# A decoder layer on one core: the final scatter in 28 tiles of 128 partitions instead of 32 of 112, with the read-back of the expert outputs in two parts

## The chip, the cores and the metric

The kernel runs on one core of one Trainium2 chip. The metric is the time of one execution in device microseconds (us). The profile is that of one execution, and its span runs from its first to its last instruction.

## What is computed

The input x has 16 batches of 224 tokens with 512 values. Three blocks are added to it: a bilinear causal mixer, a cross attention over 750 context rows with 16 heads, and a mixture of experts in which each of 32 experts picks 8 tokens of each batch. The change touches the last block alone, and of it the end:

```
probs = softmax(logits over the tokens); vals, idx = top_k(probs, 8)      # for each batch and expert
merged[b, e] = sum over k of vals[b, k, e] * x[b, idx[b, k, e]]
h = gelu([merged, 1] @ w1[e]);  o = [h, 1] @ w2[e]                        # w1[e] 513x2048, w2[e] 2049x512
out_tok[b, k, e] = o[b, e] * vals[b, k, e]
out[b, idx[b, k, e]] += out_tok[b, k, e];   x = x + out
```

Written as a product, batch b of the result is x[b] + router[b]^T @ o[b], where router[b] is 32 x 224 (the weight of each expert at each token, zero where it was not picked) and o[b] is 32 x 512.

## The kernel before

The program has three blocks: a setup, a pipeline over the 16 batches (mixer, attention, router and merging) and the experts. The last one is of interest here. `ring` is one buffer of 8 slots, each 128 partitions x 16 KB. An expert's weights are 8 MB and come in four chunks of 2 MB, one slot each: q 0 and 1 are w1, q 2 and 3 are w2. The even experts use slots 0 to 3, the odd ones slots 4 to 7. All loads are issued by SP (SyncE), whose queue is in order: a wait in it holds up everything behind it. The chunks of the last expert, 31, are issued by `weights(end, 1, ...)` in two pieces, and between them stand the 16 loads that bring x (kept in `out` by the pipeline) into the slots 0 to 3, which expert 30 has done with.

For each expert, TensorE (PE) multiplies the merged tokens by w1 (line 1573), transposes (1586), multiplies by w2 (1600) and sums four row groups (1558); VectorE (DVE) adds the bias row into `o_fin` (1515), which holds 16 rows (one for each batch) of 512. GpSimd (POOL) stores `o_fin` of the experts 0 to 30 into the DRAM tensor `o_rows` (1438, semaphore `o_stored`), and so turns rows by batch into rows by expert.

After the last expert comes the tail. SP reads `o_rows` back into `o_in` (1423), four DMAs of 31 partitions: partition r*32 + e of `o_in` holds the output of expert e for the batches 4g + r, g from 0 to 3. The row of expert 31 goes straight from `o_fin` into `o_in` in four DMAs of 4 partitions (1428). PE waits for all eight (`o_loaded`) and for `picks` (the router table in the same layout, 1407). Then it makes 32 products of 32 x 112 by 32 x 512 (1621), two for each batch: even tokens and odd tokens. The four batches of a group lie in four row groups of 32 partitions. DVE adds each product to x in the ring (1538), and ACT (ScalarE) issues one store of 112 partitions x 4 KB for each batch when both its halves are there (1472).

All three engines and the queues are ordered by semaphores as written; no scheduler moves anything.

Of the kernel before, what the change touches and what calls it, by code (L numbers as in the profile page):

```python
# [19 lines left out]
ALU = mybir.AluOpType  # L20
# [3 lines left out]
P = 128  # L24
# [48 lines left out]
def build(nc, x, ctx_in, aWq, aWk, aWo, U_b, V_b, W_b, bias_b, U_t, V_t, W_t, X_t, bias_t, alpha,  # L73
          xWq, xWkv, xWo, gate_w, gate_b, w1, w2, out):
    B, T, D = x.shape
    _, S, DC = ctx_in.shape
    R = V_b.shape[1]
    E, _, H = w1.shape
# [4 lines left out]
    TT = T // 2  # L83
# [43 lines left out]
    es = ExitStack()  # L127
    with es:
        def sem(name):
            return es.enter_context(nc.semaphore(name))  # L130

        def sb(stack, name, shape, dt=F32):
            return stack.enter_context(nc.sbuf_tensor(name, shape, dt))

        bank = [es.enter_context(nc.psum_tensor(f"bank{i}", [P, BANK], F32)) for i in range(8)]
        router = nc.dram_tensor("router", [B, E, T], F32).ap()
        o_rows = nc.dram_tensor("o_rows", [B, E, D], F32).ap()
# [291 lines left out]
        ring = sb(es, "ring", [P, SLOTS, 2 * H])  # L429
# [126 lines left out]
        def tokens(cols, t):  # L556

            return cols.rearrange("p (n t) -> p t n", t=2)[:, t, :]
# [792 lines left out]
        RW = 4  # L1351
        GB = B // RW
        o_in = sb(es, "o_in", [P, GB, D])
        picks = sb(es, "picks", [P, GB, T])

        b1_flipped = sem("b1_flipped")
        b1_ready = sem("b1_ready")
        cleared = sem("cleared")
# [13 lines left out]
        picks_loaded = sem("picks_loaded")  # L1372
        o_loaded = sem("o_loaded")
        fin_loaded = [sem(f"fin_loaded{g}") for g in range(GB)]
        scat_full = sem("scat_full")
        fin_ready = sem("fin_ready")
        fin_stored = sem("fin_stored")

        def fin(b):

            return ring[0:TT, b // RW, b % RW * 2 * D:(b % RW + 1) * 2 * D].rearrange(
                "p (t n) -> p t n", t=2)

        with nc.Block() as block:
            @block.sync
            def _(sp):
                def weights(i, e2, first, qs=range(4)):

                    e = i * 2 + e2
                    for q in qs if not first else ():  # L1390
                        slot = e2 * 4 + q
                        if q < 2:
                            sp.wait_ge(h_full, i * 2 + (e2 - 1))
                        else:
                            sp.wait_ge(o_full, i * 2 + (e2 - 1))
                        load_chunk(sp, e, q, slot)
                    if 3 not in qs:
                        return
                    if not first:
                        sp.wait_ge(o_out, i * 2 + (e2 - 1))  # L1400
                    sp.dma_start(b2_row[:, e2, :],  # L1401
                                 w2[bass.ds(e, 1), H1, :].to_broadcast([B, D])
                                 ).then_inc(b2_loaded[e2], 16)

                weights(0, 0, True)
                weights(0, 1, True)
                sp.dma_start(picks[:], router.rearrange("(g r) e t -> (r e) g t", r=RW)
                             ).then_inc(picks_loaded, 16)
                with sp.Fori(1, E // 2 - 1) as i:
                    weights(i, 0, False)  # L1410
                    weights(i, 1, False)
                end = E // 2 - 1
                weights(end, 0, False)
                weights(end, 1, False, (0, 1))
                for b in range(B):
                    if b % RW == 0:
                        sp.wait_ge(h_full if b < B // 2 else o_full, E - 1)
                    sp.dma_start(fin(b), out[b, :, :].rearrange("(p t) d -> p t d", p=TT)  # L1418
                                 ).then_inc(fin_loaded[b // RW], 16)
                weights(end, 1, False, (2, 3))  # L1420
                sp.wait_ge(o_stored, 16 * (E - 1))
                for r in range(RW):
                    sp.dma_start(o_in[r * E:(r + 1) * E - 1, :, :],  # L1423
                                 o_rows.rearrange("(g r) e n -> r e g n", r=RW)[r, 0:E - 1, :, :]
                                 ).then_inc(o_loaded, 16)
                sp.wait_ge(o_out, E)
                for g in range(GB):
                    sp.dma_start(o_in[E - 1:P:E, g, :], o_fin[g * RW:(g + 1) * RW, 1, :]  # L1428
                                 ).then_inc(o_loaded, 16)

            @block.gpsimd
            def _(pool):
                nc.gpsimd.memset(tok[:], 0.0).then_inc(cleared, 1)

                def keep_rows(i, e2):
                    e = i * 2 + e2
                    pool.wait_ge(o_out, i * 2 + (e2 + 1))
                    pool.dma_start(o_rows[:, bass.ds(e, 1), :].rearrange("b o n -> b (o n)"),  # L1438
                                   o_fin[:, e2, :]).then_inc(o_stored, 16)

                with pool.Fori(0, E // 2 - 1) as i:
                    keep_rows(i, 0)
                    keep_rows(i, 1)
                keep_rows(E // 2 - 1, 0)
                pool.wait_ge(o_stored, 16 * (E - 1))

            @block.scalar
            def _(act):
# [18 lines left out]
                with act.Fori(1, E // 2) as i:  # L1467
                    hidden(i, 0, False)
                    hidden(i, 1, False)
                for b in range(B):  # L1470
                    act.wait_ge(fin_ready, 2 * b + 2)
                    act.dma_start(out[b, :, :].rearrange("(p t) d -> p t d", p=TT), fin(b)
                                  ).then_inc(fin_stored, 16)
                act.wait_ge(fin_stored, 16 * B)

            @block.vector
            def _(dve):
# [51 lines left out]
                    add_biases(i, 1, False)  # L1529
                row_out(E // 2 - 1, 1, False)  # L1530

                for b in range(B):
                    g, r = b // RW, b % RW
                    if r == 0:
                        dve.wait_ge(fin_loaded[g], 16 * RW)
                    for t in range(2):
                        dve.wait_ge(scat_full, g * 2 * RW + t * RW + r + 1)
                        nc.vector.tensor_tensor(fin(b)[:, t, :], fin(b)[:, t, :],  # L1538
                                                bank[t * RW + r][0:TT, :], ALU.add
                                                ).then_inc(fin_ready, 1)  # L1540

            @block.tensor
            def _(pe):
# [66 lines left out]
                    expert(i, 1, False)  # L1610
                sum_parts(E // 2 - 1, 1, False)

                pe.wait_ge(picks_loaded, 16)
                pe.wait_ge(o_loaded, 16 * (RW + GB))
                for g in range(GB):
                    for t in range(2):
                        for r in range(RW):
                            if g:
                                pe.wait_ge(fin_ready, (g - 1) * 2 * RW + 2 * r + t + 1)
                            rows = slice(r * E, (r + 1) * E)  # L1620
                            nc.tensor.matmul(bank[t * RW + r][0:TT, :],  # L1621
                                             tokens(picks[rows, g, :], t), o_in[rows, g, :],
                                             start=True, stop=True).then_inc(scat_full, 1)


# [25 lines left out]
```

## Time and profile before

| | |
|---|---|
| time, median of 3 runs | 2379.69 us (2370.84, 2379.69, 2379.73) |
| time of the profiled execution | 2371.13 us |
| its span | 2369.5 us |
| busy: PE, DVE, ACT, POOL | 82%, 41%, 32%, 35% |
| experts' block begins | 1658.3 us |
| last expert's output row complete | 2308.0 us |
| first scatter product | 2339.4 us |
| last addition ends | 2363.6 us |

Times in the trace are counted from the span's start. A busy share is a mean over stages with different limits, so for a change in one stage the rows of that stage are what matters. "SPq" and "ACTq" are the DMA issues of those engines; a merged row of the timeline gives start, duration of the whole stretch, and the count. A tile's number is left out in the profile (`b_row` is `b2_row`, `bank` any bank of PSUM), and one product in f32 appears as two records.

### The profile page before, as it was taken

Reading aid. Unit: us, or ns where it says so; the run is one execution under the profiler, and the core shown is the slowest. Engines: PE = TensorE matmul, PEld = TensorE weight load, DVE = VectorE, ACT = ScalarE, POOL = GpSimd, SP = SyncE. Lnnn points to the kernel's source line nnn. Section 1 sums busy time; section 2 is a strip of 40 time slices with the busy share of each in tenths; the row PEclk is TensorE's granted clock in tenths of the full one; section 3 lists DMA queues with packets and bytes.
Section 4 is the critical chain, followed back from the end, with each engine's and each line's share of the span. In section 5 each row is a group of like instructions: output and inputs, shape, how many; then the busy total and the mean of one; then the engine's idle time right before and its main releaser. Section 6 shows DMA issues by size and latency. Waiting matters only on the chain. (4 is left out here: it accounts for less than half of the span.)

```text
span 2369.5 us, 39997 instructions
## 1 busy us (share of the span) xinstructions
PE 1953.3 (82%) x11970; PEld 1146.6 (48%) x11970; DVE 974.9 (41%) x2477; ACT 754.6 (32%) x1551; POOL 826.8 (35%) x592
## 2 busy tenths in 40 slices
PE   7789999999999999999999999986755655655633
PEld 5466666666666666666666666653211111111101
DVE  0355655656556556565565565651100000000003
ACT  2143434435444344354443443532100000000000
POOL 0245545555555455555554555543000000000000
PEclk8899999999999999999999999987877777777765
DMA  5223333242233332422433324263999999999974
GB/s 159 56 74 93 77 87 84 72 101 64 74 94 78 86 84 72 102 64 72 96 77 83 84 73 103 65 227 115 370 423 419 421 422 420 423 420 420 422 261 136
DMA packets 135414, 419.34 MB, mean 177 GB/s; under 512 B 32612, under 2 KB 74820, under 8 KB 110804
## 3 DMA queue, kind: packets, MB, share of 16 engines
q1 hardware_dynamic: 130292, 410.08, 50.9%
q10 hardware_dynamic: 4096, 7.80, 1.0%
q0 software_dynamic: 992, 1.02, 0.1%
q8 instruction: 19, 0.31, 0.1%
q14 instruction: 15, 0.12, 0.0%
HBM read 306.39 MB, written 16.15 MB: 136 GB/s over the span
## 5 line engine op out<-in xcount | busy, mean ns | idle before, releaser
L1035 DVE TENSOR_REDUCE maxes<-bank 112x1 f32<-112x376 f32 (+1 forms) x1024 | 506.8, 538 | 208.8 <-PE bank L1240 208.1
L863 ACT ACTIVATE probs<-bank 125x448 f32<-125x448 f32 x768 | 402.8, 546 | 360.4 <-PE bank L1262 353.2
L1262 PE MATMUL bank<-q_st,k_st 98*125 98x224 f32 x1536 | 384.3, 339 | 15.6 <-DMA q_st<-max_lo 9.1
L739 POOL TENSOR_TENSOR psum_keys<-psum_keys,probs 125x896 f32<-125x896 f32 x128 | 269.0, 2102 | 312.3 <-ACT probs L863 307.0
L1600 PE MATMUL bank<-ring,hid_T 128*32 128x512 f32 x1024 | 181.9, 875 | 204.3 <-DMA ring<-in_L_ffn_w 201.1
L1240 PE MATMUL bank<-k_st,q_st 96*112 96x376 f32 (+1 forms) x1024 | 324.7, 370 | 16.3 <-DVE maxes L1035 7.2
L1262 PEld LDWEIGHTS bank<-q_st,k_st 98*125 98x125 f32 x1536 | 265.6, 192 | 127.4 <-issue 74.7
L742 POOL TENSOR_TENSOR psum_keys<-psum_keys,probs 125x896 f32<-125x896 f32 x128 | 267.5, 2089 | 10.0
L1515 DVE TENSOR_TENSOR o_fin<-bank,b_row 16x512 f32<-16x512 f32 x32 | 21.7, 679 | 588.4 <-PE bank L1558 588.4
L1438 POOL DMA_DIRECT2D o_rows<-o_fin x31 | 15.3, 495 | 595.6 <-DVE o_fin L1515 595.6
L1240 PEld LDWEIGHTS bank<-k_st,q_st 96*112 96x112 f32 x1024 | 165.5, 180 | 80.5 <-DVE maxes L1035 45.4
L1600 PEld LDWEIGHTS bank<-ring,hid_T 128*32 128x32 f32 x1024 | 46.0, 153 | 315.9 <-issue 309.6
L1573 PE MATMUL bank<-ring,tok 128*32 128x512 f32 x1024 | 140.6, 673 | 69.4 <-DMA ring<-in_L_ffn_w 68.2
L1190 PE MATMUL bank<-ctx_T,wk_T 128*128 128x376 f32 (+1 forms) x512 | 185.9, 491 | 12.1 <-DVE q_lo L988 12.1
L1279 PE MATMUL bank<-probs,v 125*32 125x224 f32 x3072 | 189.7, 366 | 2.2 <-ACT probs L863 2.2
L735 POOL TENSOR_TENSOR psum_keys<-probs 125x896 f32<-125x896 f32 x64 | 134.4, 2101 | 138.8 <-ACT probs L863 130.1
L1197 PE MATMUL bank<-wv_T,ctx_T 128*125 128x512 f32 x384 | 181.0, 601 | 1.7 <-DVE k_lo L994 1.7
L1463 ACT COPY o_sb<-bank 128x512 f32<-128x512 f32 x32 | 18.8, 586 | 335.1 <-PE bank L1600 335.1
L699 POOL TENSOR_TENSOR rstd<-mean_var,small 112x2 f32<-112x2 f32 x48 | 9.4, 197 | 328.7 <-DVE mean_var L930 325.2
L1190 PEld LDWEIGHTS bank<-ctx_T,wk_T 128*128 128x128 f32 x512 | 92.3, 192 | 61.3 <-DVE q_lo L988 13.8
L994 DVE TENSOR_TENSOR k_lo<-bank,k_hi 128x376 fp32r<-128x376 f32 (+1 forms) x128 | 69.8, 546 | 123.7 <-ACT k_hi L803 122.4
L1203 PE MATMUL bank<-wo_T,o_T 128*112 128x512 f32 x256 | 115.6, 605 | 1.7 <-DVE o_T L1071 1.7
(149 smaller groups left out, 2250.5 us busy)
## 6 DMA issues: line engine op xcount, KB each, us to landing
ring<-in_L_ffn_w SPq DMA_DIRECT2D x128, 2048.0 KB, 30.5
k_st<-k_hi SPq DMA_DIRECT2D x512, 93.8 KB, 2.2
k_st<-k_lo SPq DMA_DIRECT2D x256, 93.8 KB, 2.2
q_st<-q_hi SPq DMA_DIRECT2D x512, 28.0 KB, 1.8
ctx_nat<-in_ctx SPq DMA_DIRECT2D x16, 750.0 KB
x_in<-in_x SPq DMA_DIRECT2D x16, 448.0 KB, 3.6
q_st<-q_lo SPq DMA_DIRECT2D x256, 28.0 KB, 1.9
out<-x SPq DMA_DIRECT2D x16, 448.0 KB, 7.9
```

The source lines that it names most:

```text
L735: nc.gpsimd.tensor_tensor(psum_keys[:], lo, hi, ALU.add).then_inc(keys_summed, 1)
L739: nc.gpsimd.tensor_tensor(psum_keys[:], psum_keys[:], lo, ALU.add).then_inc(pool_chain, 1)
L742: nc.gpsimd.tensor_tensor(psum_keys[:], psum_keys[:], hi, ALU.add).then_inc(keys_summed, 1)
L863: nc.scalar.activation(probs[n % 2][:, j, :], bank[5 + u % 2][0:SK, 0:2 * T], ACT.Exp, scale=SCALE).then_inc(probs_ready, 1)
L1035: nc.vector.tensor_reduce(maxes[:, j, t, c:c + 1], bank[2 + n % 3][0:TT, 0:SC[c + 1] - SC[c]], AX.X, ALU.max).then_inc(s_drained, 1)
L1190: last = nc.tensor.matmul(ps[:, 0:SC[c + 1] - SC[c]], wk_T[:, kc, kt * P:(kt + 1) * P], ctx_T[:, kc, chunk(c)], start=(kc == 0), stop=(kc ...
L1197: last = nc.tensor.matmul(ps[0:SK, :], ctx_T[:, kc, i * SK:(i + 1) * SK], wv_T[:, kc, :], start=(kc == 0), stop=(kc == KC - 1))
L1240: nc.tensor.matmul(bank[2 + n % 3][0:TT, 0:SC[c + 1] - SC[c]], q_st[slot][0:3 * HD, j, t * TT:(t + 1) * TT], k_st[slot][0:3 * HD, j, chunk ...
L1262: last = nc.tensor.matmul(bank[5 + u % 2][0:SK, kk * T:(kk + 1) * T], k_st[slot][:, j, k * SK:(k + 1) * SK], q_st[slot][:, j, :], start=Tr ...
L1279: last = nc.tensor.matmul(bank[7][j * HD:(j + 1) * HD, 0:T], v[:, 2 * c + kk, col:col + HD], p[:, j, kk * T:(kk + 1) * T], start=(c == 0 a ...
L1573: last = nc.tensor.matmul(bank[e2][c * 32:(c + 1) * 32, :], tok[:, e2, kd, :], ring[:, slot, col:col + BANK], start=(kd == 0), stop=(kd == ...
L1600: last = nc.tensor.matmul(bank[5 + e2][c * 32:(c + 1) * 32, :], hid_T[:, e2, t, c * 32:(c + 1) * 32], ring[:, slot, col:col + D], start=(t ...
```

## The change

The output is taken as 3584 rows (16 x 224) and cut in 28 tiles of 128 rows, so that tile k holds rows 128k to 128k + 127 and some tiles hold the end of one batch and the start of the next. Four batches are seven tiles (one cycle). `picks` becomes wider, with zeros around each batch's 224 columns, so that each product is 32 x 128 by 32 x 512; three tiles of each seven need two products, of two row groups, added up in one bank. A product that adds to a bank waits until the one that began it is complete (`scat_begun`). `TURN` is the order in which the tiles of a cycle are finished. The 16 loads of x become four loads of 128 partitions, three of 8 rows of 2 KB and one of 4, and the 16 stores become 28 of 128 partitions x 2 KB. `picks` is cleared by POOL and then loaded in four parts. The read-back of `o_rows` is split: experts 0 to 15 (16 partitions, four DMAs) ahead of the loads of x, and experts 16 to 30 (15 partitions, four DMAs) where all 31 were read before.

```diff
-        picks = sb(es, "picks", [P, GB, T])
+        LEAD = [r * T % P for r in range(RW)]
+        picks = sb(es, "picks", [P, GB, LEAD[1] + T + 64])
...
+        NT = B * T // P
+        PER = 2 * H // D
+        rows_out = out.rearrange("b t d -> (b t) d").rearrange("(k p) d -> p k d", p=P)
+        def fin(k):
+            return ring[:, k // PER, k % PER * D:(k % PER + 1) * D]
+        CYCLE = RW * T // P
+        TURN = [0, 2, 4, 6, 1, 3, 5]
+        def drained(k):
+            return k // CYCLE * CYCLE + TURN.index(k % CYCLE) + 1
+        def tile_at(n):
+            return n // CYCLE * CYCLE + TURN[n % CYCLE]
...
-                sp.dma_start(picks[:], router.rearrange("(g r) e t -> (r e) g t", r=RW)
-                             ).then_inc(picks_loaded, 16)
+                sp.wait_ge(cleared, 2)
+                for r in range(RW):
+                    sp.dma_start(picks[r * E:(r + 1) * E, :, LEAD[r]:LEAD[r] + T],
+                                 router.rearrange("(g r) e t -> r e g t", r=RW)[r]
+                                 ).then_inc(picks_loaded, 16)
...
-                for b in range(B):
-                    if b % RW == 0:
-                        sp.wait_ge(h_full if b < B // 2 else o_full, E - 1)
-                    sp.dma_start(fin(b), out[b, :, :].rearrange("(p t) d -> p t d", p=TT)
-                                 ).then_inc(fin_loaded[b // RW], 16)
+                def read_back(r, e0, e1):
+                    sp.dma_start(o_in[r * E + e0:r * E + e1, :, :],
+                                 o_rows.rearrange("(g r) e n -> r e g n", r=RW)[r, e0:e1, :, :]
+                                 ).then_inc(o_loaded, 16)
+                sp.wait_ge(o_stored, 16 * (E - 4))
+                for r in range(RW):
+                    read_back(r, 0, E // 2)
+                for g in range(-(-NT // PER)):
+                    sp.wait_ge(h_full if g < 2 else o_full, E - 1)
+                    n = min(PER, NT - g * PER)
+                    sp.dma_start(ring[:, g, 0:n * D].rearrange("p (k d) -> p k d", d=D),
+                                 rows_out[:, g * PER:g * PER + n, :]).then_inc(fin_loaded[g], 16)
                 weights(end, 1, False, (2, 3))
                 sp.wait_ge(o_stored, 16 * (E - 1))
                 for r in range(RW):
-                    sp.dma_start(o_in[r * E:(r + 1) * E - 1, :, :],
-                                 o_rows.rearrange("(g r) e n -> r e g n", r=RW)[r, 0:E - 1, :, :]
-                                 ).then_inc(o_loaded, 16)
+                    read_back(r, E // 2, E - 1)
...
                 nc.gpsimd.memset(tok[:], 0.0).then_inc(cleared, 1)
+                nc.gpsimd.memset(picks[:], 0.0).then_inc(cleared, 1)
...
-                for b in range(B):
-                    act.wait_ge(fin_ready, 2 * b + 2)
-                    act.dma_start(out[b, :, :].rearrange("(p t) d -> p t d", p=TT), fin(b)
-                                  ).then_inc(fin_stored, 16)
+                for n in range(NT):
+                    k = tile_at(n)
+                    act.wait_ge(fin_ready, n + 1)
+                    act.dma_start(rows_out[:, k, :], fin(k)).then_inc(fin_stored, 16)
...
+                for n in range(NT):
+                    k = tile_at(n)
+                    dve.wait_ge(fin_loaded[k // PER], 16)
+                    dve.wait_ge(scat_full, n + 1)
+                    nc.vector.tensor_tensor(fin(k), fin(k), bank[k % 8][:], ALU.add
+                                            ).then_inc(fin_ready, 1)
...
+                def scatter(k, r, first, last):
+                    if first and cycle * CYCLE + k >= 8:
+                        pe.wait_ge(fin_ready, drained(cycle * CYCLE + k - 8))
+                    if not first:
+                        pe.wait_ge(scat_begun, cycle * 3 + (k + 1) // 2)
+                    rows = slice(r * E, (r + 1) * E)
+                    at = LEAD[r] + k * P - r * T
+                    mm = nc.tensor.matmul(bank[(cycle * CYCLE + k) % 8][:],
+                                          picks[rows, cycle, at:at + P], o_in[rows, cycle, :],
+                                          start=first, stop=last)
+                    mm.then_inc(scat_full if last else scat_begun, 1)
+                for cycle in range(GB):
+                    scatter(0, 0, True, True)
+                    scatter(1, 1, True, False)
+                    scatter(3, 2, True, False)
+                    scatter(5, 3, True, False)
+                    scatter(2, 1, True, True)
+                    scatter(4, 2, True, True)
+                    scatter(6, 3, True, True)
+                    scatter(1, 0, False, True)
+                    scatter(3, 1, False, True)
+                    scatter(5, 2, False, True)
```

The order of SP's DMAs from the first two chunks of expert 31 to the end of the program, as a difference (before with -, changed with +):

```order
 L407 DMA ring<-in_L_ffn_w 128x4096 [waits h_full] x2
-L1418 DMA ring<-out 112x1024 [waits h_full]
-L1418 DMA ring<-out 112x1024 x3
-L1418 DMA ring<-out 112x1024 [waits h_full]
-L1418 DMA ring<-out 112x1024 x3
-L1418 DMA ring<-out 112x1024 [waits o_full]
-L1418 DMA ring<-out 112x1024 x3
-L1418 DMA ring<-out 112x1024 [waits o_full]
-L1418 DMA ring<-out 112x1024 x3
+L1435 DMA o_in<-o_rows 16x4x512 [waits o_stored]
+L1435 DMA o_in<-o_rows 16x4x512 x3
+L1445 DMA ring<-out 128x8x512 [waits h_full] x2
```

The four read-backs of 16 partitions now stand ahead of the loads of x, and 16 loads have become 4 (the last two wait for `o_full`, as the loads of the batches 8 to 15 did). PE's products in the changed kernel, the first cycle of seven tiles (bank n is tile n; `picks` and `o_in` of row groups 0, 1, 2, 3 in the first four rows, 1, 2, 3 in the next three and 0, 1, 2 in the last three):

```order
L1647 MATMUL bank0<-o_in,picks 128x512 [waits o_loaded,picks_loaded]
L1647 MATMUL bank1<-o_in,picks 128x512
L1647 MATMUL bank3<-o_in,picks 128x512
L1647 MATMUL bank5<-o_in,picks 128x512
L1647 MATMUL bank2<-o_in,picks 128x512
L1647 MATMUL bank4<-o_in,picks 128x512
L1647 MATMUL bank6<-o_in,picks 128x512
L1647 MATMUL bank1<-o_in,picks 128x512 [waits scat_begun]
L1647 MATMUL bank3<-o_in,picks 128x512 [waits scat_begun]
L1647 MATMUL bank5<-o_in,picks 128x512 [waits scat_begun]
```

Before, there were eight products of 112x512 in a group, each alone in its bank; now ten of 128x512 make seven tiles, and the last three follow a product in the same bank.

## Rows read from the trace of the kernel before

**Rows 1.** The page: engines' busy time; the chain that ended last, by line.

```profile
PE 1953.3 (82%) x11970; PEld 1146.6 (48%) x11970; DVE 974.9 (41%) x2477; ACT 754.6 (32%) x1551; POOL 826.8 (35%) x592
...
DMA ring<-in_L_ffn_w 20%; PE bank L1600 4%; SPq L1423 2%; PE bank L1621 1%; SPq L1428 0%; SPq L1418 0%; SPq L413 0%; DVE ring L1538 0%; DMA o_in<-o_fin 0%; SPq L1401 0%; PE bank L1573 0%; DVE adder L1480 0%; PE bank L1586 0%; DVE bank L1503 0%; ACT hid_T L1458 0%
```

**Rows 2.** Windows: stretch, length, busy us of each engine, granted clock, DMA share, GB/s.

```profile
2262.00:2282.00 20.00, 5.14 (x22) 1.51 (x22) 1.50 (x5) 1.18 (x2) 0.49 (x1) 0.63 1.04 289
2200.00:2243.00 43.00, 26.42 (x152) 7.23 (x156) 3.37 (x12) 3.54 (x6) 0.97 (x2) 0.76 1.01 421
2345.00:2367.00 22.00, 14.91 (x45) 5.34 (x44) 16.62 (x28) 0.00 (x0) 0.00 (x0) 0.67 0.94 311
2302.00:2318.00 16.00, 4.55 (x22) 0.81 (x14) 0.68 (x1) 0.59 (x1) 0.00 (x0) 0.71 0.07 25
```

**Rows 3.** Timeline of SP's DMA issues, 2240 to 2340 us.

```profile
2243.69 24.83 SPq L1418 DMA_DIRECT2D ring<-out  x16
2268.56 2.11 SPq L413 DMA_DIRECT2D ring<-in_L_ffn_w  x2
2270.71 7.32 SPq L1401 DMA_DIRECT2D b_row<-in_L_ffn_w  x1
2278.08 41.23 SPq L1423 DMA_DIRECT2D o_in<-o_rows  x4
2319.35 11.63 SPq L1428 DMA_DIRECT2D o_in<-o_fin  x4
```

**Rows 4.** Chain that ended last, in order of time, 2290 to 2345 us.

```profile
2329.29 0.61 SPq L1428
...
2329.94 0.50 SPq L1428
...
2330.48 8.73 DMA o_in<-o_fin
2339.22 0.14 issue
2339.35 3.40 PE bank L1621 x16
```

**Rows 5.** Timeline of the last expert, 2296 to 2310 us.

```profile
2299.18 6.32 PE L1600 MATMUL bank<-ring,hid_T 128*32 128x512 f32 x32 [30.67 <-DMA ring<-in_L_ffn_w]
...
2307.29 0.68 DVE L1515 TENSOR_TENSOR o_fin<-bank,b_row 16x512 f32<-16x512 f32 x1 [37.74 <-PE bank L1558]
```

**Rows 6.** Landing of a small DMA, from the page: KB each, median us.

```profile
q_st<-q_hi SPq DMA_DIRECT2D x512, 28.0 KB, 1.8
```

**Rows 7.** DMA queue in 1099 to 1101 us: only `ctx_nat`, 125 partitions, is loaded.

```profile
q1 hardware_dynamic: 225, 0.23, 32.9%
```

**Rows 8.** Timeline of DVE in the tail, 2339 to 2370 us.

```profile
2341.47 0.69 DVE L1538 TENSOR_TENSOR ring<-ring,bank 112x512 f32<-112x512 f32 x1 [33.50 <-PE bank L1621]
2342.73 4.87 DVE L1538 TENSOR_TENSOR ring<-ring,bank 112x512 f32<-112x512 f32 x8 [0.57 <-PE bank L1621]
...
2354.44 9.20 DVE L1538 TENSOR_TENSOR ring<-ring,bank 112x512 f32<-112x512 f32 x15 [0.98 <-PE bank L1621]
```

**Rows 9.** Timeline of ACT's DMA issues in the tail.

```profile
2343.45 21.66 ACTq L1472 DMA_DIRECT2D out<-ring  x16
```

**Rows 10.** Windows in the tail, columns as in rows 2.

```profile
2339.00:2341.00 2.00, 1.65 (x8) 0.85 (x12) 0.00 (x0) 0.00 (x0) 0.00 (x0) 0.50 0.03 8
...
2357.00:2359.00 2.00, 1.92 (x10) 0.72 (x11) 2.00 (x4) 0.00 (x0) 0.00 (x0) 1.00 0.94 299
```

**Rows 11.** Start of the experts' block: timeline, 1658 to 1666 us.

```profile
1658.26 0.31 POOL L1433 MEMSET tok<- 128x256 f32 x1 [16.81 <-POOLq L572]
...
1658.30 0.92 DVE L1480 COPY adder<-ident 32x32 f32<-32x32 f32 x4 [0.33 <-PEq L572]
...
1659.11 0.42 SPq L1407 DMA_DIRECT2D picks<-router  x1
1659.25 0.69 DVE L1483 COPY b_T<-bank 128x512 f32<-128x512 f32 x1
1659.97 0.20 DVE L1492 COPY tok<-merged_T 128x64 f32<-128x64 f32 x1
...
1665.40 0.90 SPq L407 DMA_DIRECT2D ring<-in_L_ffn_w  x2
```

**Rows 12.** Chain at the block's start: the first two copies of line 1480.

```profile
1658.30 0.30 DVE adder L1480
...
1658.63 0.17 DVE adder L1480
```

More of the change, by code:

```diff
@@ L1374, in build @@
         fin_loaded = [sem(f"fin_loaded{g}") for g in range(GB)]
+        scat_begun = sem("scat_begun")
         scat_full = sem("scat_full")
@@ L1377, in build @@
         fin_stored = sem("fin_stored")
-        def fin(b):
-            return ring[0:TT, b // RW, b % RW * 2 * D:(b % RW + 1) * 2 * D].rearrange(
-                "p (t n) -> p t n", t=2)
+        NT = B * T // P
[9 more added lines that the diff above has]
+            return n // CYCLE * CYCLE + TURN[n % CYCLE]
         with nc.Block() as block:
@@ L1469, in _ @@
                     hidden(i, 1, False)
-                for b in range(B):
-                    act.wait_ge(fin_ready, 2 * b + 2)
-                    act.dma_start(out[b, :, :].rearrange("(p t) d -> p t d", p=TT), fin(b)
-                                  ).then_inc(fin_stored, 16)
-                act.wait_ge(fin_stored, 16 * B)
+                for n in range(NT):
+                    k = tile_at(n)
+                    act.wait_ge(fin_ready, n + 1)
+                    act.dma_start(rows_out[:, k, :], fin(k)).then_inc(fin_stored, 16)
+                act.wait_ge(fin_stored, 16 * NT)
             @block.vector
@@ L1530, in _ @@
                 row_out(E // 2 - 1, 1, False)
[L1532 to L1540, printed above, removed]
+                for n in range(NT):
[4 more added lines that the diff above has]
+                                            ).then_inc(fin_ready, 1)
             @block.tensor
@@ L1611, in _ @@
                 sum_parts(E // 2 - 1, 1, False)
[L1613 to L1623, printed above, removed]
+                pe.wait_ge(picks_loaded, 16 * RW)
+                pe.wait_ge(o_loaded, 16 * (2 * RW + GB))
+                def scatter(k, r, first, last):
[20 more added lines that the diff above has]
+                    scatter(5, 2, False, True)
 _INS = ["x", "ctx_512", "L0_attn_Wq", "L0_attn_Wk", "L0_attn_Wo", "L0_attn_U_b", "L0_attn_V_b",
```

## The prediction

> **What bounds the kernel now.** I read the page first: PE is busy 82% of the span, but the chain that ended last names the weight loads with 20% and then two DMA issue lines of SP, 1423 and 1428 [rows 1]. So the pipeline over the batches, untouched by the change, is left aside, and the experts' block is read by windows. While weights stream, the DMA queues are full and move 421 GB/s; in the stretch in which x is loaded into the ring they are just as full (share 1.04) and move only 289 GB/s; after the last weights the rate falls to 25 GB/s and PE is idle but for the last expert [rows 2].
>
> The reader is to see what these 25 GB/s are. SP issues the four read-backs from 2278.1 on, and each next issue is held up until the one before has drained: four take 41.2 us, and the four small ones behind them 11.6 us more [rows 3]. The last of these is issued at 2330.5 and is there at 2339.2, when PE starts the scatter [rows 4]. The last expert's row, which is needed for it, was complete at 2307.29 + 0.68 = 2308.0 [rows 5]. So 31.4 us of the tail are a queue of small rows that runs on one DMA engine: 421/16 = 26 GB/s is one engine's share. The scatter then takes from 2339.35 to the span's end at 2369.5, 30.15 us: 2.1 us to the first addition, additions of 0.61 us each (4.87/8) with gaps of 0.57 to 0.98 us, the last one ends at 2363.6 [rows 8], and 5.9 us in which stores drain. The stores move 311 GB/s with the queues 94% busy [rows 2] from the first issue at 2343.45 [rows 9] on: 7.34 MB (16 x 448 KB) / 311 = 23.6 us of the 26.05 us between that issue and the end. Stores are as near to the limit there as the additions.
>
> **The change part by part.**
>
> *Loads of x, in the weights' stream.* They come ahead of the last 4 MB of weights in a queue that is never empty, so their duration counts in full. Now 7.34 MB / 289 = 25.4 us. With 128 partitions the row to go by is that of the weights, 421 GB/s, 17.4 us, but these have runs of 8 and 16 KB. Runs of 2 KB are seen in the read-back, 25 GB/s on one engine [rows 2], 400 on 16: 18.4 us. I take that: 7.0 us less, with bounds of 8.0 and, if the shape does not matter, 0.
>
> *First read-back, ahead of them.* 16 partitions x 4 x 2 KB four times are 0.52 MB, new work in the full stream. A count that 16 divides should use all 16 engines: 31 partitions used one, and 125 partitions keep the queues 32.9% busy, 5 of 16 [rows 7]. At 400 GB/s it takes 1.3 us. The dearer bound is that the engines get in each other's way when all write to few partitions, which the loads of 112 partitions hint at; four engines' worth, 100 GB/s, is 5.2 us. No row shows such a load alone; I take the middle, 3.3 us. The Trainium skill (SBUF — State Buffer, "Door 1: The DMA port swizzle") says that partitions 0 to 15 reach 4 of 16 ports, about 109 GB/s; by that alone this term would be 4.8 us and the sum 1.5 us smaller. Stream together: 7.0 - 3.3 = 3.7 us earlier, so the last expert's second product starts at 2295.5 instead of 2299.2, and its row is complete 8.8 us later [rows 5], at 2304.3.
>
> The merged loads of x have 64 runs for each engine instead of 7, so SP will stand longer in each issue. It already does (24.8 us for sixteen, rows drained at the queue's pace) [rows 3], the queue stays full meanwhile, and behind it waits only work for the same queue; cost nothing. If the queue ran dry between two issues, each would cost some 2 us.
>
> *Second read-back.* It is issued when the weights of expert 31 are queued and lands behind them: 0.49 MB on 15 engines, 1.3 us at 375 GB/s, 5 us at 100. The cover is the 8.8 us in which expert 31 is computed, so it costs nothing. Then SP issues the four 4-partition DMAs at once: 3 x 0.57 us between issues (0.61 and 0.50 with their gaps), 0.1 to react, 1.8 to 2.2 us to land (a small DMA's 1.8 [rows 6]) and 0.14 to wake PE [rows 4]. That is 4.0 us instead of 31.4: **27.4 us less**. The scatter starts at 2308.3.
>
> *The scatter itself.* Before, 8 products take 3.40 us [rows 4] at a granted clock of 0.50 [rows 10], the lower level (1.2 GHz): four row groups at once, 1.7 us for one product. Later in the tail the clock is 1.00 [rows 10], half of that. Now row groups 1 and 2 have three products for each seven tiles: 4 x 3 x 1.7 = 20.4 us at the lower level. Additions: 28 x 0.61 = 17.1 us instead of 19.5, after 2.1 us to the first and a gap of some 1.1 for the second. Counted on the order of products and drains, the last addition ends 22.7 us after the start at the lower level and 20.3 at the upper. From there one store of 256 KB remains: 0.65 us, plus the 26.05 - 23.6 = 2.45 us that a store has besides its bytes, less the issue, some 2.5 us in all: 25.2 or 22.8 us. Stores at 400 GB/s, issued from 2.8 us on: 2.8 + 2.45 + 18.4 = 23.7 us; this is the floor at the upper level. Mixed: 24.4 instead of 30.15, **5.7 us less**. Bounds: stores that stay at 311 GB/s give 2.8 + 26.05 = 28.9 (1.3 less than before); stores at 421 and the upper level some 22.8 (7.3 less).
>
> *The start of the block.* POOL clears `picks`, six times the 256 elements that take 0.31 us: up to 1.86 us, from 1658.6 to 1660.4. SP waits for it and issues four DMAs of some 0.4 us, done by 1662.1; its next issue comes at 1665.4, and PE needs `picks` only in the tail [rows 11]. So this is covered by 3.3 us. DVE is not: it copies `adder` and `tok` in that time, and PE's first product waits for `tok` at 1660.2. The first copy, which ran beside the present clearing, took 0.30 us and the next 0.17 [rows 12]. If a copy waits for the clearing's end, the `tok` copy is up to 0.5 us late, or with the `adder` copies 1.9. All weights follow from there, so it counts. I take **0.5 us more**, bounds 0 and 1.9. The Trainium skill (SBUF — State Buffer, "SBUF: two separate sides") says that DVE's fast copies and GpSimd exclude each other for a whole instruction; by that rule the `adder` copies wait too, and the sum is 1.4 us smaller.
>
> **Sum.** 3.7 + 27.4 + 5.7 - 0.5 = 36.3 us of the profiled 2371.13, that is 2334.8. That execution and one of the three runs lie at 2371, two at 2379.7, with nothing in the trace that tells them apart. The change does nothing to it, so I take the sum from the median, 2379.7 - 36.3 = **2343 us**; at the other level it would be 2335.
>
> **The rivals.**
>
> - *Shape pays nothing* (0.11). Loads of x stay at 289 GB/s and stores at 311, because of DRAM or of the 2 KB runs. For it: no row has 128 partitions with 2 KB runs or stores of 128. Against: one engine reaches 25 GB/s with 2 KB runs. Gain 36.3 - 7.0 - 4.5 = 24.8 us: 2355.
> - *The read-back is still late* (0.09). 15 partitions do not spread, or the four small DMAs are slow by themselves. 0.49 MB at 25 GB/s is 19.7 us from 2295.5: scatter at 2315.6 instead of 2308.3, gain 29.0: 2351. Slow small DMAs (8.7 us in rows 4 instead of 2) give the same 7 us. Against: that row stood behind a drained queue.
> - *The small terms go the dear way* (0.15): read-back 5.2, start 1.9. Gain 33.0: 2347.
> - *Products lose their overlap* (0.03), the slower one. Forty products one after another, because of the waits on `scat_begun` and two row groups that write to one bank: 40 x 1.7 = 68 us, the scatter takes 71 us and the time is 2390. It is slower than before from 1.44 us for one product on. Against: a wait for `scat_begun` is for a product begun 3 or more earlier, and the products before had waits between them too.
> - *Nothing to be measured* (0.02): the wait for `o_loaded` is taken over by another DMA in full, 2380.
>
> The forecast itself has the remaining 0.60, with 2335 to 2346. I count gains of 41 (all bounds good) at the lower level and 25 at the upper: **2328 to 2356** leaves out the last two rivals and some of the edges. A difference of 0.5% (12 us) is about what a measurement of this kernel can tell from no change. Faster 0.95, the same 0.02, slower 0.03.
>
> **What would show it.** In the changed trace: no stretch of 25 GB/s after the weights; line 1453 issued within 0.2 us of the last `o_fin` and PE's line 1647 some 4 us after it; the load of x near 400 GB/s and the last w2 product at 2295 to 2297; the tail's additions 0.61 us apart with gaps in each cycle; stores above 350 GB/s and under 3 us from the last addition to the end. The prediction is wrong if line 1647 starts over 8 us after the last row, if a stretch under 300 GB/s remains between 2255 and 2290, or if the seven tiles of a cycle take more than 5.5 us.

## The result and the profile after

The changed kernel takes 2342.74 us in the median of 4 runs (2342.57 to 2343.29), the kernel before 2379.09 (2370.84 to 2379.73, 4 runs): ratio 0.9856, 95% interval 0.9834 to 0.9877. That is 34 us, with 29 to 39 in the interval. The profiled execution has a span of 2341.6 us, 27.9 less than that of before.

The two differences do not agree, because the kernel before varies by more than I had seen: over the whole study its runs lie between 2369.6 and 2384.8, and within one batch of runs on one chip by 7 to 15 us. Part of this is the time at which the experts' block begins, which the change cannot touch: 1655 to 1661 us in the 14 profiled executions of all kernels. So from here on I count by stages, each as a difference of two times of one trace.

The SP queue of the changed kernel, in order of time:

```profile
2232.64 10.96 SPq L1435 DMA_DIRECT2D o_in<-o_rows  x4
2247.77 30.80 SPq L1445 DMA_DIRECT2D ring<-out  x4
2278.62 3.92 SPq L413 DMA_DIRECT2D ring<-in_L_ffn_w  x2
2282.58 1.31 SPq L1417 DMA_DIRECT2D b_row<-in_L_ffn_w  x1
2283.93 1.78 SPq L1435 DMA_DIRECT2D o_in<-o_rows  x4
2312.88 2.23 SPq L1453 DMA_DIRECT2D o_in<-o_fin  x4
```

The reader sees that the 41.2 and 11.6 us of [rows 3] are gone: the four late read-backs are issued in 1.8 us and the four small DMAs in 2.2, right behind the last expert's row. The chain that ended last shows the same place:

```profile
2281.22 22.52 DMA ring<-in_L_ffn_w
2303.75 0.14 issue
2303.89 6.54 PE bank L1623 x32
...
2312.17 0.69 DVE o_fin L1541
...
2314.61 1.77 DMA o_in<-o_fin
2316.39 0.14 issue
2316.52 4.75 PE bank L1647 x22
```

From the last row (2312.86) to the first product (2316.52) it is 3.7 us instead of 31.4 [rows 4, 5]. But the last weights land at 2303.75, 4.7 us later than before, where I had forecast 3.7 us earlier in the stream. Of these 4.7 us 1.8 are ahead of the block, 2.2 are its start and 0.7 the stream of the weights (see the table of stages). Windows of the changed kernel (columns as in [rows 2]):

```profile
2264.00:2268.00 4.00, 0.29 (x4) 0.00 (x0) 0.00 (x0) 0.00 (x0) 0.00 (x0) 1.00 1.07 129
2271.00:2286.00 15.00, 2.97 (x14) 0.84 (x6) 1.50 (x5) 1.18 (x2) 0.48 (x1) 0.73 1.05 388
2298.00:2303.00 5.00, 0.00 (x0) 0.00 (x0) 0.00 (x0) 0.00 (x0) 0.00 (x0) 0.50 0.67 82
2322.00:2340.00 18.00, 11.55 (x55) 5.23 (x52) 14.52 (x25) 0.00 (x0) 0.00 (x0) 0.92 1.01 382
```

The first is the early read-back: queues full (1.07) at 129 GB/s. The second is the load of x, 388 GB/s instead of 289. The third is the late read-back, which comes while the last packets of the weights are still under way. The fourth is the tail's stores: 382 GB/s instead of 311, and the queues full. DVE and ACT there:

```profile
2318.67 0.69 DVE L1562 TENSOR_TENSOR ring<-ring,bank 128x512 f32<-128x512 f32 x1 [5.82 <-PE bank L1647]
2320.29 16.23 DVE L1562 TENSOR_TENSOR ring<-ring,bank 128x512 f32<-128x512 f32 x27 [0.93 <-PE bank L1647]
2319.39 19.18 ACTq L1499 DMA_DIRECT2D out<-ring  x28
```

After one gap of 0.93 us the 27 other additions follow without one, and end at 2336.5; from there to the end of the span it is 5.1 us, in which stores drain. The start of the block, which in the kernel before is [rows 11]:

```profile
1660.06 0.31 POOL L1458 MEMSET tok<- 128x256 f32 x1 [16.89 <-POOLq L572]
1660.10 2.06 DVE L1506 COPY adder<-ident 32x32 f32<-32x32 f32 x4 [0.33 <-PEq L572]
...
1660.30 1.41 POOL L1459 MEMSET picks<- 128x1536 f32 x1
1661.74 1.75 SPq L1425 DMA_DIRECT2D picks<-router  x4
1662.19 0.69 DVE L1509 COPY b_T<-bank 128x512 f32<-128x512 f32 x1
1662.91 0.20 DVE L1518 COPY tok<-merged_T 128x64 f32<-128x64 f32 x1
```

The four copies into `adder` take 2.06 us instead of 0.92. The clearing runs from 1660.30 to 1661.72. It is the second copy that is held up: it lasts from 1660.43 to 1661.75, 1.32 us instead of 0.17, and everything behind it on DVE is 1.1 us later.

All kernels of the study by stages, in us, worked out from their timelines. *Start*: from the block's begin (POOL's first clearing) to SP's first weight issue in the loop. *Stream*: from there to the second product of expert 31, which waits for the last weights. *Last*: to the end of its `o_fin`. *Wait*: to the first scatter product. *Tail*: to the span's end.

| kernel | start | stream | last | wait | tail | sum |
|---|---|---|---|---|---|---|
| before | 7.1 | 633.8 | 8.8 | 31.4 | 30.2 | 711.2 |
| before again (e0) | 7.5 | 634.6 | 8.5 | 32.4 | 30.9 | 713.7 |
| changed | 9.3 | 634.5 | 9.0 | 3.7 | 25.1 | 681.5 |
| e1 split alone | 8.8 | 647.4 | 7.9 | 3.7 | 30.7 | 698.5 |
| e11 the same again | 8.7 | 645.2 | 9.0 | 3.7 | 30.3 | 696.9 |
| e10 split alone, both late | 7.4 | 641.8 | 8.2 | 3.7 | 30.8 | 691.9 |
| e2 tiles alone | 9.6 | 626.1 | 8.2 | 33.2 | 25.2 | 702.3 |
| e3 changed, both parts late | 9.7 | 629.7 | 8.1 | 3.7 | 25.2 | 676.4 |
| e6 changed, second part held | 9.7 | 631.3 | 9.0 | 3.7 | 25.1 | 678.8 |
| e4 changed, clearing later | 7.2 | 634.5 | 8.5 | 3.7 | 25.2 | 679.1 |
| e5 one read-back of 128 | 9.6 | 626.3 | 8.1 | 3.8 | 25.2 | 673.0 |
| e9 the same, 128-row load early | 9.6 | 626.4 | 8.0 | 3.8 | 25.3 | 673.0 |
| e8 the same, half the stores | 9.6 | 626.6 | 7.9 | 3.8 | 22.3 | 670.2 |
| e7 e5 and e4 together | 7.1 | 625.6 | 7.8 | 3.8 | 25.2 | 669.5 |

### The profile page after: what moved, and what is told of

The parts are those of the page before. It is cut to its first block and busy times, and to the rows that moved or that the text cites. A ratio compares the mean times of both kernels' runs of the same rounds, so it can differ in the third digit from the quotient of the medians.

```text
span 2341.6 us, 40057 instructions
## 1 busy us (share of the span) xinstructions
PE 1952.1 (83%) x11986; PEld 1148.6 (49%) x11986; DVE 973.2 (42%) x2473; ACT 754.2 (32%) x1551; POOL 827.5 (35%) x593
```

## The experiments

**e0, the kernel before once more.** No edit.

> The kernel before, unchanged, to see its two levels (2371 and 2379). Theory A: the 8 us between them lie ahead of the experts' block (setup or pipeline over the batches), so a profile at the upper level has the block's start at about 1666 instead of 1658 and the same 711 us from there to the end. Rival: they lie in the tail or in the weights' stream, and the change removed them; then the block starts at 1658 and takes some 719 us.

Ten runs lie between 2374.4 and 2377.4, and 13 of the kernel before beside them between 2371.3 and 2380.1: there are no two levels but a spread. The profiled one (2374.4) begins the block at 1659.06 and takes 713.7 us from there, 2.5 more than the first. So neither theory: some of the spread is ahead of the block, some in it. In the load of x this execution moves 266 GB/s where the first moved 289, columns as before:

```profile
2262.00:2282.00 20.00, 5.00 (x22) 1.46 (x22) 1.57 (x5) 1.18 (x2) 0.48 (x1) 0.66 1.03 266
```

**e1, the split alone.** The kernel before, with the read-back in two parts:

```diff
+                sp.wait_ge(o_stored, 16 * (E - 4))
+                for r in range(RW):
+                    read_back(r, 0, E // 2)
                 for b in range(B):
...
-                    sp.dma_start(o_in[r * E:(r + 1) * E - 1, :, :], ...)
+                    read_back(r, E // 2, E - 1)
```

> The kernel before with the read-back alone in two parts of 16 and 15 partitions, nothing else. Theory A: the wait from the last expert's row to the first product falls from 31.4 to some 3.7 us, the tail's products and stores stay at 30.1 us, and the 16-partition parts cost 5 us of the full stream, the straggling last weights another 2.5: gain some 20 us. Rival: the parts are free (1 to 2 us in the stream), gain 26 to 28 us.

2356.44 us (4 runs), ratio 0.9918 (0.9896 to 0.9939): 20 us, with 14 to 25 in the interval. The rival is out. The number is theory A's, but its sum is not: the wait is 3.7 us and the tail as before, but the stream lost 13 us, not 7.5, and the start 1.7. By stages the gain is 12.7 us against the first look at the kernel before and 15.2 against the second.

**e2, the tiles alone.** The changed kernel without its early part, and the late one 31 partitions wide:

```diff
-                sp.wait_ge(o_stored, 16 * (E - 4))
-                for r in range(RW):
-                    read_back(r, 0, E // 2)
...
-                    read_back(r, E // 2, E - 1)
+                    read_back(r, 0, E - 1)
```

> The changed kernel with the read-back of before (four DMAs of 31 partitions, all late). Theory A: loads of x some 6.5 us shorter, tail some 5 us shorter, start of the block 2.2 us longer: gain 9 us, with the 31 us wait still there and hiding nothing; the stretch of 25 GB/s ends where one engine has moved 1.0 MB, so the earlier weights may not be of use in full: then 4 to 5 us. Rival: no gain from the loads' shape and none from the stores', 0 or slower by 2.

2361.76 us, ratio 0.994 (0.9919 to 0.9961), 14 us, with 9 to 19 in the interval; the sum of the stages is 9.0 us smaller than before and 11.4 smaller than in e0. By stages the stream is 7.7 us shorter than before and the tail 5.0, the start 2.5 longer and the wait 1.8 longer. SP and PE at the place in question:

```profile
2276.61 38.83 SPq L1435 DMA_DIRECT2D o_in<-o_rows  x4
2315.49 11.53 SPq L1450 DMA_DIRECT2D o_in<-o_fin  x4
2293.97 5.73 PE L1620 MATMUL bank<-ring,hid_T 128*32 128x512 f32 x32 [25.58 <-DMA ring<-in_L_ffn_w]
```

The one engine begins its rows as soon as its share of the weights is through, so earlier weights did help: the doubt in my theory was not needed. The rival, no gain by the shape, falls.

**e3, both parts late.** The changed kernel, with the early four moved to where the other four stand:

```diff
-                sp.wait_ge(o_stored, 16 * (E - 4))
-                for r in range(RW):
-                    read_back(r, 0, E // 2)
...
                 sp.wait_ge(o_stored, 16 * (E - 1))
                 for r in range(RW):
+                    read_back(r, 0, E // 2)
+                for r in range(RW):
                     read_back(r, E // 2, E - 1)
```

> The changed kernel with both parts of the read-back late (16 and 15 partitions, eight DMAs, after the last weights are issued). Theory A: the early part costs the stream 5 us, so the last weights land 4 to 5 us earlier; the late eight take 10 us at 100 GB/s behind them against a cover of 9 us, so that 3 to 4 us of gain remain over the changed kernel: 2339 to 2340. Rival: the early placing is needed; the parts then end after the last expert and the time is 2344 to 2348.

2336.99 us (2335.67 to 2338.63), ratio 0.9838 (0.9818 to 0.9857). The stream is 4.8 us shorter than in the changed kernel, the wait is the same 3.7 us, and the sum of the stages 5.1 us smaller. The eight slow DMAs run from 2292 to 2303: the larger part of them beside the last packets of the weights, which have landed by 2298.3, and the rest under the last expert, whose row is complete at 2306.4. Late, the two parts cost 3.7 us of the stream (e3 less e2). The early place bought nothing and cost 4.8 us.

**e6, the second part held.** The changed kernel, with

```diff
+                sp.wait_ge(chunk_in[6], 16 * (E // 2))
+                sp.wait_ge(chunk_in[7], 16 * (E // 2))
                 for r in range(RW):
                     read_back(r, E // 2, E - 1)
```

> The changed kernel, with the second part of the read-back issued only when the last weights have landed. Theory A: in the changed kernel the slow 15-partition packets hold up the last stragglers of the weights by 2 to 3 us; held back, the weights land at 2301 (by the profile's clock) and the second part takes 5 us under the 9 us of the last expert: 2 to 3 us less, 2340. Rival: the stragglers are slow by themselves: 2342.7, or more if the part is then late.

2339.99 us, ratio 0.9844 (0.9812 to 0.9876); the stream is 3.2 us shorter than in the changed kernel. SP and PE:

```profile
2299.61 1.70 SPq L1435 DMA_DIRECT2D o_in<-o_rows  x4
2299.67 6.54 PE L1625 MATMUL bank<-ring,hid_T 128*32 128x512 f32 x32 [26.68 <-DMA ring<-in_L_ffn_w]
```

Issued at 2299.61, together with the product that the weights release, the part is still in time: the first scatter product comes 3.7 us after the last row. So the late part slowed the last packets of the weights. The packets of the two traces show how. In the changed kernel the last five packets of w2 (8 KB each) follow one another from 2298.02 to 2302.70 beside the read-back's and take 0.70 to 1.14 us each, 4.7 us in all; ahead of that one takes 0.31 us, which makes 1.6 us for five. The difference is 3.1 us. In e6 the last twelve take 0.31 to 0.45 us.

From e2 to the changed kernel the stream grows by 8.4 us. With e6 between them that is 5.2 us for the early part and 3.2 for the late one; with e3 between them, 3.7 for both parts late and 4.8 for moving the first one forward.

**e4, the clearing later.** The changed kernel, with

```diff
+                pool.wait_ge(tok_ready, 1)
                 nc.gpsimd.memset(picks[:], 0.0).then_inc(cleared, 1)
```

> The changed kernel, with POOL's clearing of picks held until the first tok copy is done. Theory A: the clearing held up DVE's adder and tok copies by 1.1 us, and with the first products slower behind it 2.2 us in all: the time is 1.1 to 2.2 us under the changed kernel's 2342.7. Rival: the late start has another cause (clock of the first products) and the time stays at 2342.7.

2340.32 us (2335.86 to 2342.66), ratio 0.9848 (0.9815 to 0.988): too wide to tell by the time. The start is plain, 7.2 us instead of 9.3 to 9.7 in the seven executions that have the clearing in the old place:

```profile
1655.07 0.80 SPq L1417 DMA_DIRECT2D b_row<-in_L_ffn_w  x2
1658.43 1.75 SPq L1425 DMA_DIRECT2D picks<-router  x4
1662.30 0.91 SPq L407 DMA_DIRECT2D ring<-in_L_ffn_w  x2
```

1.1 us of it is the wait of the copies. The rest is in PE's first 32 records, 5.0 us here and 6.0 to 6.3 with the clearing; but e1 and e11, which have no clearing, show 6.6 and 6.5. What these records share is the granted clock. Their 4.93 us in the kernel before had a mean granted clock of 0.73, the 5.99 in the changed one 0.60, the 6.58 in e1 0.55, the 5.04 in e4 0.72. Time by clock is 3.6 us each time: the same work, which ran at the lower level (0.50, that is 1.2 GHz) for its first 2.7, 4.8, 6.0 and 2.9 us. So of the 2.2 us 1.1 are the clearing, and the rest is a clock that rose later. This part of the rival holds. Whether the clearing has to do with the later rise is open, since e1 and e11 had it latest without one.

**e5, one read-back of 128 partitions.** The changed kernel; the row of expert 31 in `o_rows` is filled from x at the block's start, since it is read before the true one is put in its place:

```diff
+                sp.dma_start(o_rows[:, E - 1, :], x[:, 0, :]).then_inc(rows_in, 16)
...
-                sp.wait_ge(o_stored, 16 * (E - 4))
-                for r in range(RW):
-                    read_back(r, 0, E // 2)
...
-                for r in range(RW):
-                    read_back(r, E // 2, E - 1)
+                sp.wait_ge(rows_in, 16)
+                sp.dma_start(o_in[:], o_rows.rearrange("(g r) e n -> (r e) g n", r=RW)
+                             ).then_inc(rows_in, 16)
+                sp.wait_ge(rows_in, 32)
```

> The changed kernel, with one late read-back of all 128 partitions (32 rows of each batch, the row of expert 31 filled from x beforehand and overwritten by the small DMAs after) instead of the eight of 16 and 15. Theory A: 128 partitions move 1.05 MB at 385 GB/s in 2.7 us, nothing stands in the stream ahead of the last weights (5 us) and nothing slow mixes with their last packets (2 to 3 us): 7 to 8 us under the changed kernel, 2335. Rival: the read-back's shape is not what held up the last weights: within 2 us of 2342.7.

2333.3 us (2329.74 to 2334.3), ratio 0.9816 (0.9784 to 0.9848). The stream is 8.2 us shorter than in the changed kernel, the wait 0.1 us longer. Theory A holds: it is the shape of the read-back that held up the stream.

```profile
2274.84 0.37 SPq L1449 DMA_DIRECT2D o_in<-o_rows  x1
2299.18 2.29 SPq L1454 DMA_DIRECT2D o_in<-o_fin  x4
2291.05 5.59 PE L1624 MATMUL bank<-ring,hid_T 128*32 128x512 f32 x32 [25.75 <-DMA ring<-in_L_ffn_w]
```

**e9, the same bytes early, on 128 partitions.** As e5, with

```diff
+                sp.dma_start(o_in[:, 0:2, :],
+                             x.rearrange("b t d -> (b t) d").rearrange("(k p) d -> p k d", p=P)[:, 0:2, :]
+                             ).then_inc(rows_in, 16)
                 for g in range(-(-NT // PER)):
```

> As the kernel with one late read-back of 128 partitions, plus a load of 0.52 MB of x in runs of 2 KB over 128 partitions, into the same tile, where the changed kernel has its first read-back of 16 partitions; its bytes are not used. Theory A: what the early part costs is a matter of partitions, not of bytes: the stream (first weights issued to the last expert's second product) takes 626.3 + 1.4 = 627.7 us, where 16 partitions took 5.2 us more. Rival: it is bytes or runs of 2 KB among long ones, and it takes 630 to 632.

One time, 2333.75 us; the stream is 626.4 us, as without the load. 0.52 MB in the same place cost less than executions differ by (625.6 to 626.6 in e5, e7, e8 and e2), where 16 partitions cost 5.2 us. It is even less than the 1.4 us expected. The stretch of that load and of the first MB behind it, at the place where the changed kernel moved 129 GB/s:

```profile
2262.00:2266.00 4.00, 1.73 (x12) 0.51 (x16) 0.00 (x0) 0.00 (x0) 0.00 (x0) 0.85 1.01 379
```

A packet of 2 KB takes 0.09 us here and 0.28 us in the changed kernel's early read-back (medians of the packets in the two stretches). e9 differs from that read-back in two more things, the tensor it reads (x, not `o_rows`) and one DMA for four. Neither explains the cost: e5 reads `o_rows` in 128 partitions at 0.09 us a packet, and in the changed kernel the queues are full of slow packets, with no gaps between DMAs.

**e8, half the stores.** As e5, with

```diff
-                    act.dma_start(rows_out[:, k, :], fin(k)).then_inc(fin_stored, 16)
+                    act.dma_start(rows_out[:, k, 0:D // 2], fin(k)[:, 0:D // 2]).then_inc(fin_stored, 16)
```

> As the kernel with one late read-back of 128 partitions, but only the first 256 of 512 columns of each tile are stored, so the other half of the output lacks the last block. Theory A: stores at 382 GB/s set the tail's length; with half the bytes the additions do, and from the first product to the end it takes 22.5 us instead of 25.2 (last addition at 20.1, some 2.4 for the last store). Rival: something else (a store's fixed time) sets it and it stays at 25 us.

One time, 2332.93 us. The tail is 22.3 us instead of 25.2, and the queues are half busy in it:

```profile
2310.00:2328.00 18.00, 16.21 (x80) 8.64 (x72) 15.80 (x27) 0.00 (x0) 0.00 (x0) 0.87 0.51 175
```

The last addition ends 20.1 us after the first product in both; behind it there are 2.2 us here and 5.1 in e5. So the stores set the tail's end, 2.9 us beyond what one last store needs.

**e10, the split alone, both parts late.** e1 with the early four moved down as in e3.

> The kernel before with the read-back in parts of 16 and 15 partitions, both late, everything else as before. In the split alone with an early part, the loads of x moved 238 GB/s instead of 289 and the stream took 647.4 us instead of 633.8. Theory A: the early part puts the 16 engines out of step, and loads of 112 partitions are slower for it; without it they move 289 GB/s again and the stream takes 634 + 3.7 = 637 to 638 us, and the gain is 24 to 25 us. Rival: it was a bad execution, or it comes from something else in the split; then the loads stay at 240 GB/s and the stream at 642 or more.

2352.74 us (2350.9 to 2358.16), ratio 0.9894 (0.9876 to 0.9911). The stream is 641.8 us and the load of x moves 259 GB/s: between what the two theories said, so this did not settle it. Better than e1 it is, by 5.6 us of the stream.

**e11, e1 again.** No further edit.

> The split alone with its early part, once more: the loads of x of 112 partitions moved 238 GB/s there, 259 with both parts late and 289 and 266 in two executions of the kernel before. Theory A: the early part of 16 partitions puts the engines out of step and slows the 112-partition loads behind it each time: again 235 to 245 GB/s and a stream of 645 to 649 us. Rival: it is the scatter of loads of 112 partitions from execution to execution: then 255 to 290 GB/s and a stream of 640 to 643 us.

One time, 2356.95 us, with a stream of 645.2 us. In e1 and e11 the end of the early read-back is still under way until 2269, so a window from 2264, which gives 235 GB/s in e11, mixes it with the load of x. The window from 2272 to 2292 holds the load of x and, but for one small store, nothing else, first in e1, then in e11:

```profile
2272.00:2292.00 20.00, 0.68 (x4) 0.43 (x3) 1.56 (x5) 0.60 (x1) 0.48 (x1) 0.59 1.03 238
...
2272.00:2292.00 20.00, 0.33 (x3) 0.14 (x2) 1.36 (x5) 0.60 (x1) 0.48 (x1) 0.63 1.03 258
```

In e10, which has no early part, the load has begun by 2264:

```profile
2264.00:2282.00 18.00, 6.16 (x22) 1.65 (x22) 1.57 (x5) 1.18 (x2) 0.48 (x1) 0.65 1.03 259
```

So the stream is theory A's and the rate is the rival's. With the same early part the load moved 238 GB/s once and 258 the other time, and 259 without it: the loads of 112 partitions scatter, and no run shows that the early part slows them. At equal rate the early part costs 3.4 us (e11 less e10); e1's further 2.2 us go with its slower load, 30.8 us at 238 GB/s instead of 28.4 at 258.

Counted from the second look at the kernel before (634.6), whose load of x moved 266 GB/s, late parts cost 7.2 us where x is loaded by 112 partitions and 3.7 where it is loaded by 128 (e3 less e2); the early part costs 3.4 to 5.6 in the one and 4.8 in the other. Why the late parts are dearer behind loads of 112 partitions, I can only argue: those loads leave the engines out of step, and so more packets of the last weights are late. That stays open.

**e7, both mended.** e5 with the edit of e4.

> The changed kernel with one late read-back of 128 partitions and with the clearing of picks held until the first tok copy is done. Theory A: the two gains are of different stages and add up: 8.2 us (stream 626.3 instead of 634.5) and 2.2 us (7.2 instead of 9.4 from the block's start to the first weights issued), so some 10 us under the changed kernel: ratio to before 0.980. Rival: the first products take longer for another reason, and only the 1.1 us up to the first product come: 0.9805 to 0.981.

2329.87 us (5 runs, 2328.81 to 2334.13), ratio 0.9801 (0.9787 to 0.9814): the fastest kernel here, some 12 us below the changed one, with a start of 7.1 and a stream of 625.6 us. The gains of the two stages add up to 11.1 us, against 10.4 in theory A. The rival's 0.9805 to 0.981 lies inside the interval, so the time alone does not exclude it; the stage does: 2.2 us, not 1.1.

## Why the prediction was right, and where it was not

The time came out in the range and at its middle (2343 forecast, 2342.7 measured), but part of that agreement is luck. The sum of 36.3 us was made against the profiled execution, and against that the sum of the stages is 29.7 us (711.2 less 681.5), or 32.2 against e0. I then took it from a median that I read as the upper of two levels. There are no such levels; that median of three runs was high in a spread of 15 us. Without it the same sum gives 2335, 8 us under what was measured. Across the interval of the ratio the gain is 29 to 39 us, which holds the one and the other.

*The wait, 27.4 us forecast, 27.7 measured.* Right in size and by its steps: 15 and 16 partitions spread over the engines, the small DMAs are issued 0.57 us apart and land 1.8 us after the last issue. Undoing the split (e2) brings a wait of 33.2 us back. The rival "the read-back is still late" is out.

*The loads of x, 7.0 us forecast, 7.7 measured* (before less e2; 8.5 from e0). Right: 388 GB/s, near the 400 that one engine's rate gave. "Shape pays nothing" is out, here and in the stores. Partitions and the length of runs changed together, and no run separates the two.

*The first read-back, 3.3 us forecast, 5.2 measured* (e6 less e2; 4.8 as changed less e3). The dearer bound was the true one. I took the middle for want of a row; the loads of 112 partitions in [rows 2] were the hint to give more weight. The rule of the Trainium skill (SBUF — State Buffer, "Door 1: The DMA port swizzle"), by which 16 partitions reach 4 of 16 ports, stands up: 0.52 MB in 5.2 us are 101 GB/s, and the page's figure of about 109 would have given 4.8. e9 is the test of it, with the same bytes and other partitions.

*The second read-back: "lands behind them ... so it costs nothing".* This is the step that failed. I asked whether it would be late for PE, and it was not. I did not ask what it does to the work ahead of it in the queue. The 16 engines do not finish the last weights together; those that are done start on the read-back, and the others' last packets take longer beside it: five packets of the weights in a row took 4.7 us instead of 1.6 at the end. That is 3.2 us (e6).

Loads and both parts together made the stream 0.7 us longer (634.5 against 633.8) where I had 3.7 us shorter. So the tiles bring 7.7 us there, and the split takes 8.4 back. One of the prediction's own signs of being wrong came true here: 2264 to 2268 is a stretch under 300 GB/s (129) between 2255 and 2290. And the last product of w2 came at 2303.9, not at 2295 to 2297.

*The start, 0.5 us forecast, 2.2 measured,* with the bound at 1.9. The `adder` copies do wait for the clearing: the second of them ended 0.03 us behind it. The rule of the Trainium skill on the port that DVE and GpSimd share (SBUF — State Buffer, "SBUF: two separate sides") gave 1.9 us for it with a clearing of 1.86 us; the clearing takes 1.41, and the wait is 1.1 us. The trace agrees with it. The other 1.1 us are a first product at a granted clock of 0.60 where the kernel before had 0.73 (e4). I had put no term for it.

*The tail, 5.7 us forecast, 5.1 measured,* and by the floor that I named for the upper clock: stores behind additions, at 382 GB/s where I had 400. From the last addition to the end it is 5.1 us, where "under 3 us" stood among the signs. The products never set it: they kept ahead of the additions after one gap, at a granted clock of 0.92 in 2322 to 2340, where the kernel before had 0.67 [rows 2]. My mixed case gave weight to a limit at the lower level that did not appear. That products would lose their overlap, the slower rival, is out: 40 products in 17.25 us.

## What to carry to other kernels

Spread a transfer that goes through a full queue over all 128 partitions, even if some rows are read for nothing: here 16 partitions kept the queues full (share 1.07) and moved 101 GB/s where 128 moved 388, and everything behind them in the queue was late by it. Work that is issued behind a critical transfer is not yet behind it, because the engines come to it at different times; ask what it slows as well as whether it is late. And before a sum is set against a median, see how far runs of the same kernel lie apart; a gain is best counted stage by stage inside one trace.

## What had not been expected of the hardware

- A clearing of 128 x 1536 f32 by GpSimd took 1.41 us, against 0.31 for 128 x 256, so 0.86 ns for each further element (1.10 / 1280). A small copy of DVE from SBUF to SBUF that began 0.13 us after it ended 0.03 us behind it, 1.32 us long instead of 0.17.
- 0.52 MB read into 128 partitions ahead of the last weights cost nothing that could be seen (e9), into 16 partitions 5.2 us.
- A packet of 8 KB of the weights took 0.31 us by itself in a full queue, and 0.70 to 1.14 us beside the read-back of 15 partitions.
- Loads of x in 112 partitions with runs of 4 KB moved 289, 266, 259, 258 and 238 GB/s in five executions, those in 128 partitions with runs of 2 KB 384 to 388 in nine.
- Stores of 112 partitions moved 311 GB/s, of 128 partitions in half as long runs 382, in the changed kernel and in e5.
